# A transposed copy in a blockwise triangular inverse: crossbar DMA transpose in place of VectorE's block transpose

## The reference, cut to what matters

```python
def step(state, xs):
    q_t, k_t, v_t, g_t, b_t = xs
    state = state * jnp.exp(g_t)[..., None, None]
    kv = jnp.einsum('bhk,bhkv->bhv', k_t, state)
    delta = (v_t - kv) * b_t[..., None]
    state = state + jnp.einsum('bhk,bhv->bhkv', k_t, delta)
    out = jnp.einsum('bhk,bhkv->bhv', q_t, state)
    return (state, out)
```

## Time and profile before

| | |
|---|---|
| time, median of 2 runs | 2315.57 us (2313.6 to 2317.55) |
| span of the profiled execution | 2315.6 us |
| PE busy | 2275.0 us (98%) |
| DVE busy | 1953.3 us (84%) |
| ACT busy | 1326.1 us (57%) |
| POOL busy | 1204.2 us (52%) |
| block transposes L1308 | 128, 158.7 us |
| DMA queue 1 | 95.02 MB, 11.8% of 16 engines' span |

### The profile page before, as it was taken

How to read it: one execution, slowest core, us unless ns; L and a number is a source line. 1 busy time by engine, 2 the same in 40 slices (tenths; PEclk the granted TensorE clock), 3 DMA queues, 4 the chain that set the end, 5 groups by cost and what they waited for, 6 DMA issues and landing times.

```text
span 2315.6 us, 53894 instructions
## 1 busy us (share of the span) xinstructions
PE 2275.0 (98%) x20046; PEld 1784.7 (77%) x20046; DVE 1953.3 (84%) x3427; ACT 1326.1 (57%) x4125; POOL 1204.2 (52%) x1199
## 2 busy tenths in 40 slices
PE   6899999999999999999999999999999999999998
PEld 3687888878888778888788887888877888776665
DVE  5788888888888888888888888888888888885665
ACT  4565666656666656666566665666666666653110
POOL 4456555555555556555655556565565655552100
PEclk8999999999999999999999999999999999999999
DMA  4011111111001110111110111101111010120000
GB/s 140 20 38 56 38 38 38 56 38 56 27 30 56 38 56 32 44 38 56 38 48 28 38 56 38 56 20 56 38 56 38 30 46 38 38 90 1 28 10 19
DMA packets 32115, 98.46 MB, mean 43 GB/s; under 512 B 4336, under 2 KB 9840, under 8 KB 31600
## 3 DMA queue, kind: packets, MB, share of 16 engines
q1 hardware_dynamic: 31856, 95.02, 11.8%
HBM read 92.39 MB, written 2.62 MB: 41 GB/s over the span
## 4 chain that ended last, share of the span: by engine, by line
PE 97%; DVE 2%; ACT 1%; issue 1%; DMA 0%; POOL 0%; POOLq 0%; DVEq 0%; SPq 0%; ACTq 0%
PE bank L974 19%; PE bank L1001 10%; PE bank L1120 10%; PE bank L1075 5%; PE bank L548 5%; PE bank L1102 5%; PE bank L1014 5%; PE bank L1101 4%; PE bank L1034 4%; PE bank L1085 4%; PE bank L1024 4%; PE bank L1063 4%; PE bank L984 3%; PE bank L992 3%; PE bank L1040 3%; PE bank L1110 3%
## 5 line engine op out<-in xcount | busy, mean ns | idle before, releaser
L1278 DVE SCALAR_TENSOR_TENSOR conv<-bank,cw_all,conv 128x511 f32<-128x511 f32 (+2 forms) x768 | 564.7, 742 | 45.2 <-ACT conv L1170 40.3
L974 PE MATMUL bank<-xT,w_kh 128*128 128x512 f32 x1024 | 531.0, 602 | 2.8 <-ACT kraw L1198 1.8
L1170 ACT ACTIVATE conv<-bank,cw_all 128x512 f32<-128x512 f32 x256 | 176.8, 691 | 245.4 <-PE bank L974 245.4
L1314 DVE TENSOR_TENSOR N<-bank,lev 128x512 f16<-128x512 f32 x384 | 258.9, 674 | 56.7 <-PE bank L1024 56.7
L1215 ACT ACTIVATE X<-bank 128x512 f16<-128x512 f32 x384 | 229.0, 596 | 100.6 <-PE bank L1034 100.6
L1120 PE MATMUL bank<-wo,ogT 128*128 128x256 f32 x1024 | 268.7, 385 | 0.0
L887 POOL TENSOR_TENSOR keys<-kraw,kfac 128x1024 f32<-128x1024 f32 x64 | 121.4, 1897 | 277.8 <-PE bank L1085 277.5
L1001 PE MATMUL bank<-w_kh,xT 128*128 128x256 f32 x1024 | 263.9, 391 | 0.1
L926 POOL TENSOR_TENSOR ms<-ms,epsq 128x8 f32<-128x8 f32 x64 | 12.8, 199 | 388.7 <-ACT og L1230 388.7
L1024 PEld LDWEIGHTS bank<-X,mhiT 128*128 128x128 f16 x3072 | 135.9, 98 | 101.0 <-issue 46.5
L1034 PEld LDWEIGHTS bank<-N,XT 128*128 128x128 f16 x3072 | 131.8, 98 | 106.3 <-DVE N L1314 52.8
(11 more groups left out here) (181 smaller groups left out, 5651.2 us busy)
## 6 DMA issues: line engine op xcount, KB each, us to landing
egb<-rows SPq DMA_DIRECT2D x64, 512.0 KB, 4.9
ecb<-rows SPq DMA_DIRECT2D x64, 512.0 KB, 4.0
w_kh<-w_heads SPq DMA_DIRECT2D x16, 768.0 KB, 6.0
wo_raw<-w_out SPq DMA_DIRECT2D x16, 256.0 KB, 6.2
xT<-x_cols SPq DMA_DIRECT2D x4, 512.0 KB, 5.9
xT<-gate_up SPq DMA_DIRECT2D x1, 2048.0 KB, 7.7
ecb<-x_rows SPq DMA_DIRECT2D x3, 512.0 KB, 3.7
out<-og SPq DMA_DIRECT2D x3, 512.0 KB, 2.9
```

Of the source, the lines that this page charges most:

```text
L974: mm = pe.matmul(PB[j % 2][:, :], w[:, k, g * P:(g + 1) * P], xT[:, k, b * SEQ:(b + 1) * SEQ], start=(k == 0), stop=(k == KT - 1))
L1170: act.activation(conv[:, g, :], PB[i % 2][:, :], ACT.Copy, scale=cw_all[:, head, g * TAPS + 3:g * TAPS + 4]).then_inc(s_tap, 1)
L1278: dve.scalar_tensor_tensor(conv[:, g, m:], PB[j % 2][:, 0:SEQ - m], cw_all[:, head, g * TAPS + 3 - m:g * TAPS + 4 - m], conv[:, g, m:], op ...
L1314: dve.tensor_tensor(blocks(N[:, i], i, 0), packed(IB[1 - i % 2], i), blocks(lev[:, 1 + i:2 + i, :], i, 0).broadcast_to(shape), ALU.mult).t ...
```

## The change

Level 0's transposed copy of X is now made by a DMA with transpose, issued by SyncE, from X to XT, both in SBUF. `turned` of index 0 leaves VectorE's list; `turned` of index 1 stays. PE's `growx` of level 1 waits for the DMA (s_xf), that of level 2 for VectorE (s_xv). SyncE gets a list of its own, in which the egb load of the body four ahead comes first, then the flip of the body two ahead, then the ecb load of the body three ahead, then the weights.

```diff
-        ("conv", 3, 3), ("acc", 0, 0), ("conv", 4, 3), ("turned", 0, 2), ("join", 1, 2), ("s", 1, 1), ("conv", 5, 3),
+        ("conv", 3, 3), ("acc", 0, 0), ("conv", 4, 3), ("join", 1, 2), ("s", 1, 1), ("conv", 5, 3),
...
+    "sync": [
+        ("egs", 0, 4), ("flip", 0, 2), ("ecs", 0, 3), ("weights", 0, 3),
+    ],
...
-            for n in range(BODIES):
-                for dst, i, s_load, s_free, m in ((egb, 0, s_eg, s_scan, 2), (ecb, 1, s_ec, s_qe, 1)):
...
+            def run(name, i, n):
+                if name == "egs":
                     if n > 1:
...
+                        sp.wait_ge(s_scan, 2 * (n - 1))
+                    decay_rows(egb, 0, n, s_eg)
+                elif name == "ecs":
+                    if n > 1:
+                        sp.wait_ge(s_qe, n - 1)
+                    decay_rows(ecb, 1, n, s_ec)
+                elif name == "flip":
+                    sp.wait_ge(s_x, 6 * n + i + 1)
+                    sp.dma_start_transpose(XT[:, :, :], flat(X)).then_inc(s_xf, 16)
...
-                    if 0 < i <= TURNED:
-                        pe.wait_ge(s_xv, TURNED * n + i)
+                    if i == 1:
+                        pe.wait_ge(s_xf, 16 * (n + 1))
+                    if i == 2:
+                        pe.wait_ge(s_xv, n + 1)
```

More of the change, by code:

```diff
@@ L209, in build_kernel @@
         s_xv = sem("s_xv")
+        s_xf = sem("s_xf")
         s_resp = sem("s_resp")
@@ L815, in _, with decay_rows @@
             sp.wait_ge(s_rowd, 32)
-            for n in range(BODIES):
-                for dst, i, s_load, s_free, m in ((egb, 0, s_eg, s_scan, 2), (ecb, 1, s_ec, s_qe, 1)):
-                    if n > 1:
[L819 to L823, removed]
+            def decay_rows(dst, i, n, loaded):
+                sp.dma_start(dst[:, n % 2], rows[i, CELLS * n:CELLS * (n + 1)].rearrange("x t -> (x t)")
+                             .unsqueeze(0).broadcast_to([P, CELLS * P])).then_inc(loaded[n % 2], 16)
+            def run(name, i, n):
+                if name == "egs":
+                    if n > 1:
+                        sp.wait_ge(s_scan, 2 * (n - 1))
[7 more added lines that the diff above has]
+                    sp.dma_start_transpose(XT[:, :, :], flat(X)).then_inc(s_xf, 16)
+                elif name == "weights":
+                    if n % B == 1 and n // B + 1 < KH:
+                        weights(n // B + 1)
+            for name, i, n in rounds(ORDER["sync"]):
+                run(name, i, n)
             moe_loads(sp)
```

## The result

| | before | after |
|---|---|---|
| median | 2315.57 us (2 runs) | 2364.7 us (2 runs, 2364.28 to 2365.11) |
| span of the profiled execution | 2315.6 us | 2363.4 us |
| PE busy | 2275.0 us | 2283.5 us |
| DVE busy | 1953.3 us | 1887.2 us |

The ratio is 1.021, 95% interval 1.0191 to 1.0229. The change makes the kernel slower, by 49 us; whether by more than 2% the interval leaves open. The prediction had 98 us.

What follows compares the result with a forecast made beforehand. The prediction took TensorE's stream as the bound: 62 bodies x 1.5 us of stall = 93, first two bodies 4, tail 1, gain 0, so 2315.6 + 98 = 2414 us, 4.2% slower, range 2320 to 2500 us.

Steps and rivals of the forecast that it cites:

- What bounds the kernel: TensorE's own stream sets the time, without idle time in 1940 us; relieving VectorE of 79 us gains 0.
- The place and the form of the stall: TensorE waits for the DMA at growx 1, for what exceeds 2.61 us of cover: 1.5 us a body.
- F: Transposing DMA's time from issue to landing, taken as 4.0 us between 2.1 and 5.4, at twice its bytes' cost.
- The upper bound: Eight squares each cost SyncE 0.43 us of issue, then 2.0 us for a small transfer: landing after 5.4 us.
- likeliest case: Stall of 0.7 to 2.3 us at growx 1 without clock falls, 2362 to 2465 us; chance 0.46.
- The first two bodies, 4 us: While the pipeline fills, cover at growx 1 is about 0.5 us less: 2 x 2.0 = 4 us.
- The end: In the last body the x_rows load stands behind the flip and delays VectorE's next transpose: 1 us, once.
- SyncE's order, 0: On SyncE, egb issued some 10 us earlier and ecb 0.5 to 3 us later cost 0.
- Hidden anyway: At growx 1 the transfer lands within the cover, or nearly, so time stays at 2315 to 2320 us; chance 0.27.
- Squares in line: The DMA's eight squares are issued one after another, stalling growx 1 by 2.9 us: 2505 us; chance 0.14.
- The clock falls too: Stalls drop TensorE's clock to half in every second body, 51 us more: 2465 us; chance 0.11.
- Faster: VectorE's relief reaches TensorE's weight loads, which wait 52.8 us for N: 2263 us; chance 0.02.

Runs made afterwards that it cites:

- experiment 2: Kernel before without VectorE's transposed copy of level 0 and nothing in its place, growx 1 waiting only for N: 2315.2 us, ratio 1.0002.
- Experiments 3: Changed kernel with a plain 256 KB DMA from X to XT in place of the transposing one: 2322.88 us, 1.0038 of the kernel before.
- 4: Changed kernel with the DMA transposing only four cells (128 KB) and VectorE the other four: 2326.36 us, 1.005 of the kernel before.
- 5: Changed kernel with a second transposing DMA of 128 KB, to a scratch buffer, issued ahead of each real one: 2459.23 us, 1.0629 of the kernel before.
- 8: Changed kernel with join 0 and growx 0 moved 0.9 us earlier on TensorE, VectorE and ScalarE: 2330.7 us, 1.0071 of the kernel before.
- experiment 14: Changed kernel with the chain started earlier on three engines and the x_rows load ahead of the last flip: 2325.87 us, 1.0047 of the kernel before.
- experiment 13: Changed kernel with only the x_rows load moved ahead of the last flip: 2362.91 us, 1.0209 of the kernel before.
- experiment 1: Kernel before with only SyncE's new order, both transposed copies staying with VectorE: 2316.86 us, ratio 1.0009.
- experiment 7: Changed kernel with TensorE's proj 4 moved ahead of growx 1: 2364.64 us, 1.022 of the kernel before.
- 15 to 18: Four kernels where the DMA makes level 5's copy in place of TensorE's growt, with entries reordered to cover waits: 2347.37, 2377.06, 2397.68 and 2403.78 us.
- experiment 9: Changed kernel with the x_rows load and the expert weights issued ahead of the last flip: 2370.65 us, 1.0238 of the kernel before.
- experiment 6: Kernel before, copies by VectorE, plus two 128 KB transposing DMAs a body to scratch, for which no matmul waits: 2319.53 us, 1.0024.

## Why the prediction was wrong, by its steps

**What bounds the kernel: right.** TensorE's stream sets the time. Taking VectorE's 79 us away gave 2315.2 us (experiment 2); VectorE's busy time fell by 66 us, since a part of each transpose had overlapped its neighbours' rows. The weight loads' wait for N is still 50.9 us there, where it was 52.8: this relief hardly reaches it, and what it would be worth no run shows.

**The place and the form of the stall: right.** Growx 1, released by the DMA, in every body; D is F plus wakes minus the cover of 2.61 us. Experiments 3, 4, 5 and 8 move F, the issue and the start one at a time, and the body follows each.

**F, the term that failed.** The stall was the right one, its size came from a wrong flight time. I took 4.0 us, near the middle of 2.1 to 5.4 and argued from "twice its bytes". It is 3.06. The wakes are 0.16 and not 0.1, so D is 3.06 + 0.16 - 2.61 = 0.61 in place of 1.5 us. Between the X of body 2 and of body 62 the sum had 60 x 1.5 = 90 us; 36.6 and the 7.5 of late landings were measured. That is 46 of the 50 us by which the spans' difference was overestimated (98 against 47.8). The upper bound was the weak end: it took the price of SyncE's issue eight times, 3.4 us, where the whole issue takes 1.23, and put a whole small transfer behind it. The step behind "twice its bytes" was wrong as well. The landing time of a 512 KB load holds time to move the bytes, while a flip of 256 KB differs from a plain copy of 256 KB only in packets of 256 B, 0.6 us in all. The lower bound's 1.35 us fixed share was closer (1.46 us for the plain copy, 1.65 for the flip: the time to the first packet and that behind the last).

The estimate from the Trainium skill's page "DMA: Bandwidth & Descriptors" (its sections on the anatomy of a DMA and "Latency and other measured facts": 261 GB/s and a fixed cost of about 2.0 us) gave F 3.0 us, D 0.5 and 2348 us, and this trace agrees in the sum: 3.06 and 0.61. I had its figure beside a guess of mine and went by the guess. In its parts it does not agree: the 256 KB moved in 1.41 us, 186 GB/s, with a fixed part of 1.65 us, and the two deviations cancel. That is luck, the more so since that page of the Trainium skill fits its 2.0 us on DMAs issued by GpSimd, and gives 261 GB/s for a transpose whose middle dimension is not contiguous (350 to 400 GB/s for the contiguous case). Eight times the figure of the page "VectorE: DVE Perf Modes" of the Trainium skill (section "The three transpose paths", 1309 ns for a square of 128 x 128) would have been 10.5 us. Measured are 3.06 us for eight squares and 2.41 for four: between four and eight, each costs 0.16 us.

**Late landings: missing in the sum.** One F for all bodies; 11 have 3.49 to 4.25 us. Late landings cost some 7.5 us here and make most of what experiment 14 still has over before (9.4 us between the X of body 2 and of body 62). Without them the result would lie under 2%. They also brought the time, by luck, just into the 2362 to 2465 us of my likeliest case, though F and D both lie below its 3.2 to 4.8 and 0.7 to 2.3 us.

**The first two bodies, 4 us: measured -0.2.** The stall came as said (growx 1 starts 1.2 and 1.1 us later after X). But in the profiled executions, one of each, the clock was at 0.50 for longer before the change than after it, which would make up for that; it was not isolated. Stretch of 55 to 120 us, before and after (clock: third number from the end):

```profile
55.00:120.00 65.00, 56.83 (x517) 43.13 (x516) 52.84 (x84) 35.82 (x104) 31.58 (x33) 0.92 0.05 18
```

```profile
55.00:120.00 65.00, 54.53 (x518) 40.66 (x517) 51.15 (x82) 35.61 (x104) 31.95 (x33) 0.97 0.20 58
```

**The end: right in sum, not in its parts.** I had two bodies' D and 1 us for the load, 4.0 us; measured are 3.9. But the load behind the flip, whose place was named, makes 3.4 of them (experiment 13), and the two stalls nearly nothing.

**SyncE's order, 0: right** (experiment 1). egb is issued at 1027.15, 10.7 us ahead of the flip.

**The rivals.** "Hidden anyway" needed F below 2.6 us; a plain copy would have it (experiment 3). Its wider form, F under 3.2 us and the time within 2%, is nearly what happened: D 0.61, F 3.06, and 2.1%. "Squares in line" fell with experiment 4. "The clock falls too": not in a steady body at a stall of 0.6 us. At 1.9 us (experiment 5) it does fall, in 6 of 60 bodies and not in every second one; about 1.8 us each, near the 1.6 priced, make some 11 us and not 51. "Faster" fell with experiment 2.

## What to carry to other kernels

A transfer that replaces an engine's work on a dependent chain was paid here by its latency minus the cover, in every round, while the relief of the engine bought nothing. First look whether the relieved engine is waited for at all. When a latency is known only between far bounds, don't take the middle: build it from its parts (issue to first packet, packets, landing), each from its nearest row, and price each end apart. To hide a longer latency, try an earlier start of the chain on all its engines (experiment 8); in experiment 7 and in 15 to 18 an entry moved in one engine's list only moved the stall.

## What was new of the hardware

- A crossbar flip of 256 KB between two SBUF buffers lands 3.06 us after its issue, one of 128 KB 2.41 us, a plain copy of 256 KB 2.29 us. It travels as 1024 packets of 256 B.
- SyncE is held 1.23 us by the issue of the flip, 1.19 us for half of it, 0.47 us for the plain copy; issued behind four weight loads of 3.5 MB together it was 4.48 us (experiment 9).
- 11 of 64 transfers on the path landed 0.4 to 1.2 us late. Each had an instruction-fetch packet in flight; of the 53 others 8 had one and 45 had none. That it is the cause was not shown.
- Some 69,600 further packets cost the engines nothing in a steady body as long as no one waited for them (experiment 6).
- The granted clock fell to 0.50 in 6 of 60 steady bodies at a stall of 1.9 us a body, and in none at 0.6 us (experiment 5 and after).
